# Turning two small operands of a low-rank matmul kernel on VectorE in 32 by 32 blocks, with one product moved

## The reference

```
base = x @ W.T
logits = x @ Wr.T + 5 * onehot(language)           # 8 experts
gates = softmax over the two largest of 8, else 0
c = base + 2 * sum_e gates[e] * (x @ A[e].T) @ B[e].T      # rank 16 each

base2 = c @ Wf.T + bf
gates2 = softmax(c @ Wrf.T)                        # 4 experts
f = base2 + 2 * sum_e gates2[e] * (c @ Af[e].T) @ Bm[e].T  # rank 8 each
out = x + f
```

## Time and profile before

| | us |
|---|---|
| Time, median of three runs | 332.79 (332.75 to 333.36) |
| The profiled execution's own time | 332.64 |
| Its span, first to last instruction | 330.9 |
| TensorE busy | 325.8 |
| VectorE busy | 214.2 |
| ScalarE busy | 119.3 |

### The profile page before, as it was taken

The page is one execution under the profiler, slowest core; times in us unless marked ns, Lnnn a source line. Parts: engine busy times, 40 slices in busy tenths (PEclk is TensorE's granted clock), DMA queues, the critical chain, the costliest instruction groups (busy, mean ns, idle before and its releaser), DMA issues.

```text
span 330.9 us, 5486 instructions
## 1 busy us (share of the span) xinstructions
PE 325.8 (98%) x2056; PEld 321.9 (97%) x2056; DVE 214.2 (65%) x473; ACT 119.3 (36%) x238; POOL 1.3 (0%) x11
## 2 busy tenths in 40 slices
PE   7999999999999999999999999999999999999996
PEld 7999999999999999999999999999999999999995
DVE  3989999898899878156347635724763572565421
ACT  4962836494247224023212412402331250322111
POOL 1000000000000000000000000000000000000000
PEclk9999999999999999999999999999999999999999
DMA  7997000000000304202500600240070043003003
GB/s 260 418 410 256 2 2 0 2 0 2 0 2 0 130 0 159 95 0 63 190 0 0 243 10 0 85 168 0 0 254 0 0 129 125 0 1 127 1 0 127
DMA packets 8188, 26.96 MB, mean 81 GB/s; under 512 B 1038, under 2 KB 2062, under 8 KB 8176
## 3 DMA queue, kind: packets, MB, share of 16 engines
q1 hardware_dynamic: 8032, 26.80, 22.3%
q10 hardware_dynamic: 144, 0.01, 0.0%
HBM read 18.42 MB, written 8.39 MB: 81 GB/s over the span
## 4 chain that ended last, share of the span: by engine, by line
PE 98%; DVE 0%; POOL 0%; issue 0%; POOLq 0%
PE sums L1037 97%; PE sums L1221 1%; PE sums L1246 1%; DVE rows L1023 0%; POOL ident L436 0%; DVE ident_r L650 0%; POOL ident L434 0%; POOLq L436 0%; POOLq L1320 0%
## 5 line engine op out<-in xcount | busy, mean ns | idle before, releaser
L1037 PE MATMUL sums<-b_high,a_high 128*128 128x256 f32 (+1 forms) x224 | 45.8, 288 | 0.0
L1037 PE MATMUL sums<-b_low,a_high 128*128 128x256 f32 (+1 forms) x224 | 45.8, 288 | 0.0
L1037 PE MATMUL sums<-ct_low,st_high 128*128 128x428 f32 x128 | 45.6, 357 | 0.0
L1037 PE MATMUL sums<-ct_high,st_high 128*128 128x428 f32 x128 | 45.6, 356 | 0.0
L1037 PE MATMUL sums<-ct_high,st_low 128*128 128x428 f32 x128 | 45.6, 356 | 0.0
L1037 PE MATMUL sums<-b_high,a_low 128*128 128x256 f32 (+1 forms) x224 | 45.6, 287 | 0.0
L1037 PEld LDWEIGHTS sums<-b_high,a_high 128*128 128x128 f32 x224 | 35.3, 191 | 0.2
L1037 PEld LDWEIGHTS sums<-b_low,a_high 128*128 128x128 f32 x224 | 35.3, 191 | 0.0
L1037 PEld LDWEIGHTS sums<-b_high,a_low 128*128 128x128 f32 x224 | 35.1, 191 | 0.0
L1037 PE MATMUL sums<-t_high,s_high 128*128 128x384 f32 x96 | 32.4, 338 | 0.0
L1037 PE MATMUL sums<-t_high,s_low 128*128 128x384 f32 x96 | 32.4, 337 | 0.0
(11 more groups left out here) (133 smaller groups left out, 667.8 us busy)
## 6 DMA issues: line engine op xcount, KB each, us to landing
stage<-tokens SPq DMA_DIRECT2D x14, 512.0 KB, 3.5
out<-rows SPq DMA_DIRECT2D x14, 512.0 KB, 3.7
in<-part SPq DMA_DIRECT2D x7, 585.0 KB, 7.6
in<-part SPq DMA_DIRECT2D x4, 777.0 KB, 14.9
in<-part SPq DMA_DIRECT2D x4, 265.0 KB, 17.4
rows<-tokens SPq DMA_DIRECT2D x2, 512.0 KB, 15.7
out<-rows SPq DMA_DIRECT2D x4, 192.0 KB, 2.1
c_plain<-gate_proj SPq DMA_DIRECT2D x1, 544.0 KB, 17.4
```

The lines of the kernel that those rows point to most:

```text
L1037: return nc.tensor.matmul(out_, lhs, rhs, start=start, stop=stop, skip_group_check=True)
```

## The change

TensorE no longer turns u and v. VectorE does it with its transpose of blocks of 32 by 32: `turn` takes 32 tokens by 32 columns of both tiles in one instruction and writes the turned block to its place in `ut_plain` or `vt_plain`, which lie in SBUF where PSUM banks were used before. u takes 16 such instructions: the four that make the first 32 rows stand in front of the sum out of bank B (L969 of before), the other twelve behind it. v takes four.

What follows v changes too. ScalarE copies the turned v twice into `vt` (rows 0 to 31 and 64 to 95), VectorE makes the low part of rows 32 to 63, behind the split of the next tile of x; the low part is now the second of three groups of rows, and the mask on `mix` moves with it. The rows of ones are written once, at the start.

On TensorE the seventh product now stands in front of the narrow `lora`, and the narrow mixing behind `lora` on B. On VectorE the second sum out of bank B moves in front of the maximum; on ScalarE the rounding of the next tile of x moves in front of the exponentials.

```diff
@@ ScalarE, pair
                 act.wait_ge(u_turned, j + 1)
-                copy(ut_high[:, :, :], ut_psum).then_inc(ut_high_ready, 1)
+                copy(ut_high[:, :, :], ut_plain[:, :, :]).then_inc(ut_high_ready, 1)
+
+                if not last:
+                    act.wait_ge(p2_done, j + 1)
+                    round_x(j + 1, 0)
...
-                if not last:
-                    act.wait_ge(p2_done, j + 1)
-                    round_x(j + 1, 0)
-
                 act.wait_ge(v_turned, j + 1)
-                copy(vt[:, :, :], vt_psum).then_inc(vt_ready, 1)
+                copy(vt[2 * ER2:3 * ER2, :, :], vt_plain[0:ER2, :, :])
+                copy(vt[0:ER2, :, :], vt_plain[0:ER2, :, :]).then_inc(v_rounded, 1)
@@ VectorE
-            nc.vector.memset(v_rows[:, :, 3 * ER2:3 * ER2 + 2], 1.0).then_inc(ones_made, 1)
+            nc.vector.tensor_scalar(vt[3 * ER2:MIX, :, :], ident[3 * ER2:MIX, :].unsqueeze(1).to_broadcast([2, 2, P]),
+                                    0.0, 1.0, ALU.mult, ALU.add).then_inc(ones_made, 1)
...
+            def turn(dst, src, rows_from, columns_from):
+
+                return nc.vector.transpose(dst[columns_from:columns_from + BLOCK, :, rows_from:rows_from + BLOCK],
+                                           src[rows_from:rows_from + BLOCK, :, columns_from:columns_from + BLOCK])
+
+            def turn_u(i):
+
+                for q in range(BLOCKS):
+                    ins = turn(ut_plain, u, q * BLOCK, i * BLOCK)
+                return ins
@@ VectorE, pair
                 if first:
                     split_block(B21, C21)
+                dve.wait_ge(u_ready, j + 1)
+                turn_u(0)
...
                     .then_inc(u2_read, 1)
+                for i in range(1, BLOCKS):
+                    last_turn = turn_u(i)
+                last_turn.then_inc(u_turned, 1)
...
-                for t in range(2):
-                    ins = nc.vector.tensor_copy(
-                        v_rows[:, t, 0:2 * ER2].bitcast(F32R).rearrange("p (a c) -> p a c", a=2),
-                        v[:, t, :].unsqueeze(1).to_broadcast([P, 2, ER2]))
-                link(ins)
-                nc.vector.tensor_tensor(v_rows[:, :, 2 * ER2:3 * ER2], v[:, :, :], v_rows[:, :, 0:ER2], ALU.subtract)\
-                    .then_inc(v_ready, 1)
...
+                for q in range(BLOCKS):
+                    ins = turn(vt_plain, v, q * BLOCK, 0)
+                ins.then_inc(v_turned, 1)
                 if not last:
                     split_x(j + 1, 0)
+                dve.wait_ge(v_rounded, j + 1)
+                low_part(vt[ER2:2 * ER2, :, :], vt_plain[0:ER2, :, :], vt[0:ER2, :, :]).then_inc(vt_ready, 1)
@@ TensorE, pair
-                pe.wait_ge(u_ready, j + 1)
-                for t in range(2):
-                    last = nc.tensor.transpose(ut_psum[:, t, :], u[:, t, :], ident[:, :])
-                last.then_inc(u_turned, 1)
...
-                pe.wait_ge(v_ready, j + 1)
-                for t in range(2):
-                    last = nc.tensor.transpose(vt_psum[:, t, :], v_rows[:, t, :], ident[:, :])
-                last.then_inc(v_turned, 1)
```

More of the change, by code:

```diff
@@ L70, in adaln_ffn_kernel @@
     S2, S1, S3, S4 = range(4)
-    BANK_A, BANK_B, BANK_C, BANK_D, BANK_T, BANK_U, BANK_V = 3, 0, 1, 2, 4, 6, 7
+    BANK_A, BANK_B, BANK_C, BANK_D, BANK_T = 3, 0, 1, 2, 4
+    BANK_WARM = 7
     FIRST_BANK = (0, 0, 1, 1)
@@ L122, in adaln_ffn_kernel @@
         v = sb("v", [P, 2, ER2])
-        v_rows = sb("v_rows", [P, 2, MIX])
         vt = sb("vt", [MIX, 2, P], F32R)
@@ L197, in adaln_ffn_kernel @@
         c0_sum = c_plain[:, C22, 0, :]
+        ut_plain = c_plain[:, C12, 0, 0:2 * P].rearrange("p (t c) -> p t c", t=2)
+        vt_plain = c_plain[0:ER2, C12, 1, 0:2 * P].rearrange("p (t c) -> p t c", t=2)
         here_1 = [sem(f"here_1_{k}") for k in range(HALF)]
@@ L282, in adaln_ffn_kernel @@
         y_exp_ready = sem("y_exp_ready")
-        v_ready = sem("v_ready")
         v_turned = sem("v_turned")
+        v_rounded = sem("v_rounded")
         vt_ready = sem("vt_ready")
@@ L442, in _ @@
             pool.wait_ge(mask_made, 1)
-            nc.gpsimd.memset(mix_is_low[ER2:2 * ER2, :], 1.0).then_inc(mask_made, 1)
+            nc.gpsimd.memset(mix_is_low[2 * ER2:3 * ER2, :], 1.0).then_inc(mask_made, 1)
             pool.wait_ge(mask_made, 2)
@@ L915, in _ @@
             STEPS = 14
+            BLOCK = 32
+            BLOCKS = P // BLOCK
+            def turn(dst, src, rows_from, columns_from):
[5 more added lines that the diff above has]
+                return ins
             def pair(j, first=False, last=False):
@@ L970, in pair @@
                     .then_inc(u2_read, 1)
+                for i in range(1, BLOCKS):
+                    last_turn = turn_u(i)
+                last_turn.then_inc(u_turned, 1)
                 dve.wait_ge(ut_high_ready, j + 1)
-                low_part(ut_low[:, :, :], ut_psum, ut_high[:, :, :]).then_inc(ut_low_ready, 1)
+                low_part(ut_low[:, :, :], ut_plain[:, :, :], ut_high[:, :, :]).then_inc(ut_low_ready, 1)
                 if first:
                     split_t(T4, C11)
+                if not first:
+                    dve.wait_ge(stored[1], 16 * j)
+                dve.wait_ge(p7_done, j + 1)
+                nc.vector.tensor_tensor(rows[:, 1, WIDE:2 * WIDE], bank(BANK_B), rows[:, 1, 0:WIDE], ALU.add)\
+                    .then_inc(u3_read, 1)
                 dve.wait_ge(y_small_ready, j + 1)
@@ L1045, in _ @@
             for _ in range(WARM_UP):
-                last = mm(sums[:, BANK_V, :].rearrange("p (a c) -> p a c", a=4), ident_r[:, :],
+                last = mm(sums[:, BANK_WARM, :].rearrange("p (a c) -> p a c", a=4), ident_r[:, :],
                           ident_r[:, :].unsqueeze(1).to_broadcast([P, 4, P]), start=True, stop=True)
@@ L1227, in pair @@
                 of_x(BANK_A, 0, 1, cw_high[B21], cw_low[B21], False).then_inc(p2_done, 1)
-                pe.wait_ge(ut_low_ready, j + 1)
-                for t in range(2):
-                    last = lora(BANK_T + t, t, 2 * WIDE, MCOLS)
-                last.then_inc(y_small_ready, 1)
                 if first:
@@ L1237, in pair @@
                 of_s(BANK_B, S3, t_high[T3], t_low[T3], False).then_inc(p7_done, 1)
+                pe.wait_ge(ut_low_ready, j + 1)
+                for t in range(2):
+                    last = lora(BANK_T + t, t, 2 * WIDE, MCOLS)
+                last.then_inc(y_small_ready, 1)
                 lora(BANK_A, 0, 0, WIDE)
@@ L1252, in pair @@
                 of_x(BANK_B, 1, 1, t_high[T4], t_low[T4], False).then_inc(p4_done, 1)
+                lora(BANK_B, 1, 0, WIDE)
+                pe.wait_ge(ones_made, 1)
                 pe.wait_ge(vt_ready, j + 1)
```

3 lines of the change are left out of this document (removed).

## The result

The changed kernel takes 339.69 us (median of 5 runs, 338.88 to 340.1) against 332.79 us before (median of 5, 332.03 to 333.36): a ratio of 1.0202, 95% interval 1.0189 to 1.0214. It is slower by 6.9 us; the forecast was 337.6 us, 4.8 us slower. The profiled execution took 339.37 us, with a span of 337.5.

A forecast was written before the change was run, and what follows sets the result against it. TensorE, busy for 98% of the span, was taken to bound the kernel. From 332.64 us, 2.80 more in seven later pairs and 2.13 in the first, savings already netted, gave 337.6 us; range 329.4 to 340.6.

The forecast's parts named there:

- What is removed: TensorE's transposes of u and v, two places in eight pairs at 0.22 us: 3.52 us, all on the path.
- The value of p: p, time from one VectorE turn of u to the next: 0.24 us; costs more than saved from 0.215 on.
- The rivals with overlap: u's 16 turns overlap: 0.15 gives 329.8 us, chance 0.31; partly, 0.18 to 0.22, chance 0.10. Against: partition groups change.
- The longer turn: Rival: a turn outlasts a plain instruction of its size, p = 0.30, 345.5 us; chance 0.09.
- The rule of the Trainium skill: VectorE instruction reading or writing another 32-partition group waits for all earlier ones; would hold all but one of 16 turns.
- ScalarE's copy: Copy of the turned u behind the last turn: 0.39 us, price left unchanged although its source is now SBUF.
- TensorE leaving its wait: Start of the narrow matmuls after ut_low: 0.03 plus 0.13 of the 0.19 weight load, 0.16 us.
- v in the middle pairs: Turned v ready for mixing at 237.96, TensorE there at 239.13: 1.17 us to spare, no cost.
- The rounding ahead of the exponentials: ScalarE's rounding of the next x, 1.06 us, ends at 232.97 before the maximum at 233.70, so it hides.
- The first pair: TensorE waits 0.75 for turned u, 0.28 before the fourth product, 1.54 before mixing; less 0.44, 2.13 us more.
- TensorE loses speed by waiting: Rival: waits lower TensorE's clock, adding to the slow cases; nothing showed it, so no chance of its own.

The follow-up runs named there:

- e6: Changed kernel with the fifth product also in front of the narrow matmuls behind the first pair, and the third in front of the mixing: 332.4 us, ratio 0.999.
- e1: Changed kernel with all 16 turns of u reading and writing the first 32 partitions, into a spare place; output not the reference's: 330.65 us, ratio 0.9923.
- e5: Changed kernel with the narrow matmuls in front of the seventh product again, all turns kept: 366.27 us, ratio 1.099.
- e4: Changed kernel with only v turned on VectorE; u transposed by TensorE, narrow matmuls in front of the seventh product, as before: 331.31 us, ratio 0.9944.
- e7: As e6, with two splits of the first pair, of C21 and T4, given to GpSimd: 333.36 us, ratio 1.0022.
- e8: As e7, with the mixing in front of the third product again in the last pair: 332.68 us, ratio 0.9998.
- e2: As e1, but each of the 16 turns covers all 128 partitions, every block inside its own group: 330.3 us, ratio 0.9931.

## Why the prediction was right, and where it was short

The sign, the mechanism and the places of all the waits were as forecast, and the time lay in the range; 2.1 us were missing. That the time lay in the range says little by itself, since the range was 11 us wide and held both signs; what was right is the step between turns and what hangs on it.

- **What is removed** (16 x 0.22 = 3.52): right. In e6, without waits in the middle, a pair is 0.43 shorter for 0.44 forecast.
- **The value of p** (0.24, from the nearest row's duration and a third of a handover): 0.25, the duration of 0.235 and 0.015 between turns. The step itself, "each begins only when the one before has ended", is what the chain shows. Sixteen times 0.01 is 0.16 us a pair. The rivals with overlap would have been right for turns inside one group (e1: 0.13, and a gain of 2.3 us for 2.8 forecast at 0.15), and fall here for the reason that stood against them. (By the prediction's own steps the first pair's wait at 0.15 is 0.77 and not 0.69; in e1 it was 0.87.) The longer turn falls by the duration of 0.235, that of the plain row of its size. The rule of the Trainium skill ("VectorE: DVE Perf Modes", section "Two Vector instructions with no wait between them") has been borne out on both sides, the read one and the written one: 0.25 against 0.13 us.
- **ScalarE's copy** (0.39, "I leave its price"): 0.42. Another 0.03.
- **TensorE leaving its wait** (0.16, then steps as usual): mis-sized both ways. It starts 0.05 after ut_low has ended (236.50 + 0.42 to 236.97), which is 0.11 better, but the first matmul behind the wait is followed by the second only 0.25 later, not 0.13, which gives 0.12 back. I had the uncovered weight load in front of the matmul. Its record begins together with the matmul's, and the delay stands behind it; that the load is the reason isn't shown.

```profile
236.97 0.19 PEld L1057 LDWEIGHTS sums<-c_high,ut_high 128*128 128x128 f32 x1 [1.11 <-DVE ut_low L659]
```

- Together 0.16 + 0.03 - 0.11 + 0.12 = 0.20: a pair costs 0.61 more than before and not 0.40. Over the six steps that is 1.3 us, the bulk of the miss; the last pair's end is 0.41 later, as forecast. Another 0.4 is the first pair, and 0.45 lies outside the span and between the profiled execution and the median.
- **v in the middle pairs** (1.17 to spare, nothing lost): right; vt ends at 242.45 and is used at 243.69, with no idle time in front. **The rounding ahead of the exponentials**: hidden, as forecast.
- **The first pair** (2.13 more, waits of 0.75, 0.28 and 1.54): 2.51 more up to the second pair. The mixing matmuls stand at 127.66 for 127.33 forecast; the waits are 0.69 and 1.40, and the fourth product begins at 123.39 for 123.14, some 0.25 late for the 0.28 forecast. The rest is p again, 16 and then 4 times, and the slow first matmul behind each wait.
- **TensorE loses speed by waiting** ("nothing shows what one would do ... nothing of its own"): right for this change, where a wait of 0.80 leaves the clock at 1.00, but not for longer ones: in e5 waits of 2.76 to 2.89 us came with 3.3 us or more at about 0.5 in seven of eight pairs. My own expectation of e5 failed on just that.

What stays open, beside the clock in e5's first pair: why in e4, e6, e7 and e8 14 of the 40 runs (and one of e2's five) have 2.4 to 3.0 us of time around the span, where the others have 1.7 to 2.1 and all runs of before about 1.8. It is part of what separates e6's median (0.5 below before) from its profiled span (1.0 below).

## What to carry to other kernels

Cost a transpose by blocks of 32 partitions on VectorE at its full duration per instruction, 0.25 us here, because neighbours that change their group of 32 partitions don't overlap; a few of them hide, sixteen in a row on the way to TensorE's next operand need more independent work in front of it than one product. When an engine that bounds the kernel gives work away, count what stands between the request and the operand's use, and move independent products there before counting the saving: here the same turns cost 33 us with no product moved (the slower clock included), 7 with one and nothing with three. Choose the form per stage, since first and last pairs have less cover than the middle ones.

## What the runs showed of the hardware that was not expected

- In e5, waits of TensorE of 2.76 to 2.89 us came with 3.3 us, twice 6.7, at the lower clock (0.50 to 0.51 granted) in seven pairs; one of 2.77 us, in the first pair, did not. In the changed kernel, waits of 0.80 and, in the first pair, 1.40 us were not followed by any slice below the full clock.
- Not only turns wait for their neighbour: in the changed kernel's fifth pair `vt`, a subtraction that writes from row 32 on, and the sum behind it each began 0.03 us after the one before had ended, where neighbours from the same row overlap by 0.08.
- With GpSimd at a split with two inputs in SBUF, a sum of VectorE with two inputs in SBUF took 4.76 us in place of 1.75, that is, it did its work once GpSimd was done. GpSimd's second split (117.17 to 120.36) lay beside block turns, which have one input, and these took 2.99 as ever. This agrees with the Trainium skill ("SBUF — State Buffer", section "Who interferes with whom"), which says that a VectorE instruction with two SBUF inputs contends with a GpSimd one that reads SBUF, and one with a single input doesn't.
- The same split takes 3.45 us on GpSimd and 1.75 on VectorE.
